# Two of sixteen output tiles leave VectorE: a GRU plus block-attention kernel on one Trainium2 core

## The reference

```python
def reference(x, cond, W_ih, W_hh, b_ih, b_hh, rms_weight, Wk, Wo, ln_gamma, ln_beta):
    # 1: a GRU over the 64 steps, state starts at cond
    def cell(h, x_t):
        gi, gh = x_t @ W_ih + b_ih, h @ W_hh + b_hh
        r, z = sigmoid(gi_r + gh_r), sigmoid(gi_z + gh_z)
        n = tanh(gi_n + r * gh_n)
        return (1 - z) * n + z * h
    x = x + gru(x)                                   # (32, 64, 512)
    # 2: attention over 8 blocks of 8 steps each
    block = x.reshape(32, 8, 8, 512).sum(axis=2)
    keys = block @ Wk.T;  keys = keys / rms(keys) * rms_weight
    attn = softmax(keys @ cond[1])                   # over the 8 blocks
    proj = (attn @ block) @ Wo.T                     # one row per sequence
    y = x + proj[:, None, :]
    # 3: layer norm, and the residual
    return x + (y - mean(y)) / sqrt(var(y) + 1e-6) * ln_gamma + ln_beta
```

## Time and profile before

| what | us |
|---|---|
| median of 3 runs | 374.22 (373.96 to 374.42) |
| profiled execution, its own time | 373.8 |
| its span (first to last recorded event) | 371.8 |
| what lies around the span in that execution | 2.0 |
| TensorE busy | 361.5 (97% of the span) |
| VectorE busy | 266.2 (72%) |
| ACT busy | 157.6 (42%) |

### The profile page before, as it was taken

One profiled execution on the slowest core, in us unless ns is written; L12 is line 12 of the kernel. 1 busy time (PEld: TensorE's weight loads), 2 busy tenths in 40 slices (PEclk: granted clock), 3 DMA queues, 4 the chain that ended last, 5 costly groups with the idle time before them and its releaser, 6 DMA issues.

```text
span 371.8 us, 9814 instructions
## 1 busy us (share of the span) xinstructions
PE 361.5 (97%) x3272; PEld 212.2 (57%) x3272; DVE 266.2 (72%) x1142; ACT 157.6 (42%) x505; POOL 16.6 (4%) x49
## 2 busy tenths in 40 slices
PE   8998999999999999999999999999999999999895
PEld 5545655566665556665556666555666655444572
DVE  2937667677676778676768767676867676888787
ACT  4402325262534344352526263434445255865510
POOL 5013000000000000000000000000000000100100
PEclk9999999999999999999999999999999999999999
DMA  8995544424232322324142323232232412111138
GB/s 285 409 329 138 175 103 147 109 60 101 72 99 71 90 66 62 99 56 113 38 104 48 99 71 99 71 97 71 51 98 60 109 43 71 51 30 33 28 136 317
DMA packets 28101, 40.06 MB, mean 108 GB/s; under 512 B 3121, under 2 KB 19121, under 8 KB 28081
## 3 DMA queue, kind: packets, MB, share of 16 engines
q1 hardware_dynamic: 28080, 39.79, 36.7%
HBM read 19.60 MB, written 4.19 MB: 64 GB/s over the span
## 4 chain that ended last, share of the span: by engine, by line
PE 86%; DMA 5%; DVE 3%; issue 2%; SPq 1%; ACT 1%; POOLq 0%; DVEq 0%; POOL 0%
PE gates_ps L622 42%; PE gi_ps L591 36%; DMA gcx<-in_w_ih_dram 2%; DMA w_hh<-in_w_hh_dram 2%; PE gi_ps L604 1%; PE third_ps L622 1%; PE keys_ps L622 1%; PE fourth_ps L622 1%; SPq L276 1%; PE first_ps L761 1%; PE keys_ps L742 1%; DMA h_tok<-hist 1%; PE gi_ps L695 0%; PE small_ps L761 0%; POOLq L29 0%
## 5 line engine op out<-in xcount | busy, mean ns | idle before, releaser
L622 PE MATMUL gates_ps<-w_hh,turned 128*32 128x384 f32 x1920 | 167.2, 489 | 0.4 <-DVE turned L836 0.3
L622 PEld LDWEIGHTS gates_ps<-w_hh,turned 128*32 128x32 f32 x1920 | 56.4, 109 | 84.7 <-issue 56.0
L591 PE MATMUL gi_ps<-w_ih_hi,xt_hi 128*128 128x384 f32 x240 | 86.8, 363 | 0.0
L591 PE MATMUL gi_ps<-w_ih_hi,xt_lo 128*128 128x384 f32 x240 | 80.7, 338 | 0.0
L591 PE MATMUL gi_ps<-w_ih_lo,xt_hi 128*128 128x384 f32 x240 | 79.7, 334 | 0.0
L478 ACT ACTIVATE rz<-gates_ps 128x256 f32<-128x256 f32 x59 | 22.7, 385 | 128.7 <-PE gates_ps L622 128.7
L898 DVE TENSOR_TENSOR rz<-gates_ps,rz 128x128 f32<-128x128 f32 x59 | 17.2, 292 | 75.7 <-ACT rz L478 75.6
L591 PEld LDWEIGHTS gi_ps<-w_ih_hi,xt_hi 128*128 128x128 f32 x240 | 44.9, 187 | 37.5 <-issue 36.9
L591 PEld LDWEIGHTS gi_ps<-w_ih_lo,xt_hi 128*128 128x128 f32 x240 | 45.1, 188 | 0.0
L591 PEld LDWEIGHTS gi_ps<-w_ih_hi,xt_lo 128*128 128x128 f32 x240 | 44.9, 187 | 0.0
L836 DVE STREAM_TRANSPOSE turned<-hist 128x32 f32<-128x32 f32 x189 | 36.1, 216 | 2.1
(11 more groups left out here) (230 smaller groups left out, 298.1 us busy)
## 6 DMA issues: line engine op xcount, KB each, us to landing
gi<-gi_tok SPq DMA_DIRECT2D x60, 192.0 KB, 3.4
x1t<-in_x_t_dram SPq DMA_DIRECT2D x16, 256.0 KB, 3.3
gcx<-in_x_tok_dram SPq DMA_DIRECT2D x16, 256.0 KB, 3.2
h_tok<-hist SPq DMA_DIRECT2D x64, 64.0 KB, 2.2
out_dram<-gcx SPq DMA_DIRECT2D x16, 256.0 KB, 2.1
gcx<-in_w_ih_dram SPq DMA_DIRECT2D x4, 768.0 KB, 6.6
w_hh<-in_w_hh_dram SPq DMA_DIRECT2D x4, 768.0 KB, 9.4
wo_t<-in_wo_t_dram SPq DMA_DIRECT2D x1, 1024.0 KB, 5.4
```

What stands on the lines that cost most here:

```text
L591: mm = pe.matmul(gi_ps[tok][:, 0:G3], a[:, k, :], w[:, k, gi_cols(j)], start=(m == 0), stop=(m == 3 * NJ - 1))
L622: mm = pe.matmul(gates_bank(t)[j * B:(j + 1) * B, P:], before[:, k * B:(k + 1) * B], chunk(w_hh, k, j), start=False, stop=(k == NJ - 1), s ...
```

## The change

Quads 7 and 11 no longer go through `finish`. ACT makes a 128x128 matrix with rstd of the quad's tokens on the diagonal (`make_diag`: the identity times a scale per partition). TensorE multiplies `gcx[:, quad, :]` by it and accumulates in the quad's bank, on top of what lay_x1 and add_gcp put there (`lay_tokens`). ACT copies the bank to `gcx[:, quad, :]` (`copy_out`). SyncE and TensorE wait for the new semaphore `pe_out_ready` for these quads, and for `out_ready` at a count without them for the others. Apart from that, the last group's add_gcp comes once for four quads, after lay_x1 of 12, 13, 14 and 15, where it came twice for two quads each.

```diff
+        pe_quads = (7, 11)
+        diag_of = [end[:, (40 + m) * P:(41 + m) * P] for m in range(len(pe_quads))]
...
+        def pe_outs(quad):
+            return sum(q <= quad for q in pe_quads)
+        def dve_outs(quad):
+            return quad + 1 - pe_outs(quad)
...
             for quad in range(NQ):                                  # SyncE
-                sp.wait_ge(out_ready, quad + 1)
+                if quad in pe_quads:
+                    sp.wait_ge(pe_out_ready, pe_outs(quad))
+                else:
+                    sp.wait_ge(out_ready, dve_outs(quad))
                 sp.dma_start(out[:, quad, :], gcx[:, quad, :]).then_inc(out_stored, 16)
...
             keep_rstd(1)                                            # ACT
             root(2)
+            def make_diag(quad):
+                act.wait_ge(rstd_kept, (1, 2, 3, 3)[quad // Q])
+                act.activation(diag_of[pe_outs(quad) - 1], ident[:], ACT.Copy, scale=rstd_tok[:, quad:quad + 1]
+                               ).then_inc(diag_made, 1)
+            def copy_out(quad):
+                act.wait_ge(tokens_laid, pe_outs(quad))
+                act.activation(gcx[:, quad, :], out_ps[quad % len(out_ps)][:], ACT.Copy).then_inc(pe_out_ready, 1)
+            make_diag(pe_quads[0])
+            copy_out(pe_quads[0])
             keep_rstd(2)
+            make_diag(pe_quads[1])
+            copy_out(pe_quads[1])
...
-                if quad >= len(out_ps):                             # TensorE, lay_x1
-                    pe.wait_ge(out_ready, quad - len(out_ps) + 1)
+                if quad - len(out_ps) in pe_quads:
+                    pe.wait_ge(pe_out_ready, pe_outs(quad - len(out_ps)))
+                elif quad >= len(out_ps):
+                    pe.wait_ge(out_ready, dve_outs(quad - len(out_ps)))
...
+            def lay_tokens(quad):
+                pe.wait_ge(diag_made, pe_outs(quad))
+                pe.wait_ge(gcx_ready, quad + 1)
+                pe.matmul(out_ps[quad % len(out_ps)][:], diag_of[pe_outs(quad) - 1], gcx[:, quad, :], start=False, stop=True,
+                          skip_group_check=True).then_inc(tokens_laid, 1)
...
             add_gcp(1)
+            lay_tokens(pe_quads[0])
             lay_x1(8)
             lay_x1(9)
             pe.wait_ge(rstd_kept, 2)
             lay_rstd(2)
             lay_x1(10)
             lay_x1(11)
             add_gcp(2)
-            for first in (0, Q // 2):
-                for g in (first, first + 1):
-                    lay_x1(3 * Q + g)
-                add_gcp(3, (first, first + 1))
+            lay_tokens(pe_quads[1])
+            for quad in range(3 * Q, NQ):
+                lay_x1(quad)
+            add_gcp(3)
...
             for quad in range(Q, 2 * Q):                            # VectorE
-                finish(quad)
+                if quad not in pe_quads:
+                    finish(quad)
             centre_tokens(NQ - 1)
             for quad in range(2 * Q, NQ):
-                finish(quad)
+                if quad not in pe_quads:
+                    finish(quad)
```

More of the change, by code:

```diff
@@ L165, in gru_block_attention @@
         u_laid, out_ready, out_stored = sem("u_laid"), sem("out_ready"), sem("out_stored")
+        diag_made, tokens_laid, pe_out_ready = sem("diag_made"), sem("tokens_laid"), sem("pe_out_ready")
         def wait(eng, s, value):
```

## The result

The changed kernel takes 376.19 us in the median of 6 runs (375.59 to 376.96), the kernel before 374.53 beside it (6 runs, 373.96 to 375.04). The ratio is 1.0049, 95% interval 1.0036 to 1.0063, or 1.8 us (1.3 to 2.4) more. Slower, as forecast; the forecast was 376.2, +1.98. That the medians agree to 0.01 us is partly luck: the loss came out a little smaller than forecast, and the kernel before, measured again, 0.31 us slower than the 374.22 that the forecast started from.

A forecast was written before the change was run, and what follows sets the result against it. The prediction took packed TensorE as the bound of the last stage, VectorE almost level; +0.66 us (TensorE) and +1.32 (two more finishes behind the last group) make +1.98, from 374.22 to 376.2 us, range 375.4 to 377.0.

The forecast's parts named there:

- The sum: Whole last stage: +0.66 us on TensorE plus +1.32 for two more finishes behind the last group, +1.98 in all.
- TensorE is packed: TensorE in the last stage runs without slack, so added matmuls delay the last group: +1.80 - 1.14 = +0.66 us.
- The joined transposes: lay_x1 of quads 12 to 15 in one row on TensorE: 1.96 us against 2.04 before.
- The row behind the 0.90: Key products of the recurrence on TensorE, taken as the same form as lay_tokens: 1.80 / 2 = 0.90 us each.
- The rule of the Trainium skill on overlap: TensorE weight loads overlap matmuls in flight only in another row group; each lay_tokens would cost 1.06, the sum 0.32 more.
- VectorE's savings turn into waiting: Two finishes of 0.66 us saved on VectorE become waits for add_gcp, some 1.55 ahead of quad 8, 1.9 before finish(12).
- Four finishes behind the last group: On VectorE after the last add_gcp, four finishes are left in place of two: +1.32 us, called the largest term.
- priced the stores at nothing: Final stores: 0.69 us each on the DMA engines, at most 0.1 us built up, tail after the last finish unchanged.
- ACT at no cost: make_diag (0.28 us) and copy_out (0.67) on ACT cost nothing, hidden by TensorE's stream.
- rival A: Faster: VectorE is the bound and its two finishes come off whole, 1.32 us less, 372.9; chance 5%.
- B (hidden in the loads' idle time): No change: token matmuls cost TensorE's array nothing beside the add_gcp groups; +0.2 us, 374.4; chance 5%.
- C (a new bank wait): Slower still: lay_x1(14) and (15) wait for finishes 8 and 9; with 0.8 us beyond the slack, 377.0; chance 8%.

The follow-up runs named there:

- quads 13 and 15: Changed kernel with quads 13 and 15 in place of 7 and 11 by diagonal matmul and ACT copy: 376.47 us, ratio 1.0058.

## Why the prediction was right

**The sum.** Its two terms add up to the measured stretch: +0.62 on TensorE (0.66 predicted) and +1.30 for two more finishes behind the last group (1.32 predicted) are the 1.92. The range was added up wrongly: its own terms give 375.65 to 377.05, not 375.7 to 376.8. The result lies well inside either.

**TensorE is packed: right.** The starts follow each other from 359.61 to 368.31. From the start of add_gcp(1) to the end of the last group there are 9.29 us, against 8.67 before (359.17 to 367.84): +0.62 for a predicted +0.66. The start before, in the same columns:

```profile
359.17 0.69 PE L761 MATMUL gates_ps<-w_hh 32*128 32x512 f32 x1
```

The parts: lay_tokens takes 0.96 to 0.97 against 0.90 taken, with 1.06 as the upper end; but the lay_x1 behind it takes 0.43 (365.92 to 366.35), not 0.49, and its first load had begun ahead of it. That is 0.90 to 0.91 net. The joined transposes take 1.83 with that, for 1.96. The row behind the 0.90 was not quite of the form: its stationary has 96 columns, not 128. Between two pieces of full-array work, with quads 13 and 15, a lay_tokens takes 0.86 (366.15 to 367.01), the lower end of the prediction; it takes 0.95 to 0.97 where a row-tiled group stands on one side of it.

The rule of the Trainium skill on overlap that the prediction took (TensorE: Matmul & The Clock Gate, "The mechanism") is not what these rows show: the load of lay_x1(8) begins at 361.21, while the next matmul starts only when lay_tokens' second pass is through, at 361.64, and both use the whole array. The same section of the Trainium skill also has the queue pull a load ahead when it goes to a background weight buffer, which the prediction left out; with that the rows agree. The two token matmuls cost less than the 1.06 that would have followed from the first rule.

**VectorE's savings turn into waiting: right.** 1.55 us ahead of quad 8 (predicted 1.55) and 1.81 ahead of quad 12 (1.9).

**Four finishes behind the last group: right in size, incomplete as a cause.** They begin 0.07 after the group's end and are over at 371.69, and the two more cost 1.30 (2.79 from the group's end to the last finish's, 1.49 before). But I named the joined group as the largest term, as if undoing it would win that back. The runs show otherwise: two pairs instead cost +1.81, nearly the same, because TensorE's last group then ends 1.19 later (370.00 - 353.74 = 16.26 after the stage's start, for 15.07). Alone, joining costs +0.46. The two parts of my sum are not two parts of the change; what costs is, for the most part, the 1.8 us of matmul, whichever way the group is cut. And the stores need those 0.69 us each themselves: taking finishes off this tail does not shorten it, as quads 13 and 15 showed. The prediction priced the stores at nothing because they had kept pace; they keep pace with finishes 0.66 apart, and hardly faster. For the changed kernel that was right: from the last finish to the span's end there are 2.5 us, as before.

**ACT at no cost: right.** copy_out takes 0.60, make_diag 0.39 rather than 0.28, both over before anyone asks: make_diag(7) at 359.54 for lay_tokens at 360.68, copy_out(7) at 362.44 for lay_x1(13) at 366.35. The Trainium skill's advice to empty PSUM with both engines (TensorEngine Tiling (Array Packing), "PSUM Bottleneck") stood for rival A; here emptying was not the bound, and the way to ACT led over TensorE, which was.

**The rivals.** A (faster) is out: the group ends 9.29 after add_gcp(1)'s start where it would need 7.3. B (hidden in the loads' idle time) is out: the matmul takes its full time from start to start. C (a new bank wait) did not occur in the changed kernel; it occurred, at about 0.3 (lay_x1(15) 0.74 after lay_x1(14)), in the kernels with a joined group and at most one token matmul ahead of it, where TensorE is early. The kernel before with float32r add_gcp, where TensorE is early too, has it as well (365.12 after 364.37).

## What to carry to other kernels

Moving work off an engine that looks busy pays only if the engine that receives the means (here two matmuls for a diagonal) has time before the end; read that from start-to-start distances and from when each wait's releaser was really done, not from the idle time named beside the weight loads. Here three resources run nearly level up to the end: VectorE at 0.66 us a tile, the stores at 0.69, and TensorE, which needs 0.84 a tile in group 2 (3.37 us from lay_x1(8) at 360.24 to lay_x1(12) at 363.61) and started ahead. Relieving TensorE therefore showed the stores behind it after 0.5 to 0.8 us, so price all three for every variant. And a term of a sum is not the price of undoing that part: run each half alone.

## What the runs showed that I had not expected

Behind a row-tiled group, a 128x512 matmul in float32r takes 0.33 us from its start to the next, against 0.96 in fp32: about a third and not half. An fp32 copy of 128 columns with a per-partition scale takes ACT 0.39 us where one without takes 0.28 (the first writes to SBUF and the second to PSUM, so the scale is not shown to be the reason). When stores pile up, SyncE's issue of a store grows from 0.34 to 0.64 us and its landing from 2.1 to 3.0.
